# Gathers of a two-layer graph network: foreign rows passed over by a bound, and a memset of 260 columns in place of 300 ahead of each gather

## The reference, cut to what matters

```
h = relu(layernorm(x)); x = x + L0(h)     # graph attention, 8 heads of 16
h = relu(layernorm(x)); x = x + L1(h)     # q, k, v attention over edges, edge bias, layernorm
L0: e = leaky(a_src[src] + a_dst[dst]);            alpha = softmax of e over edges with one dst
    out[dst] = sum alpha * h[src]
L1: s = q[dst].k[src]/4 + edge_attr @ We + be;     attn = softmax of s over edges with one dst
    out[dst] = (sum attn * v[src]) @ Wo + bo
```

## Time and profile before

| | us |
|---|---|
| median of 3 runs | 1489.5 |
| lowest and highest | 1488.92, 1489.5 |
| the profiled execution | 1486.06 |
| its span | 1484.3 |
| POOL busy | 1190.4 |
| TensorE (PE) busy | 980.2 |
| VectorE (DVE) busy | 929.5 |
| ScalarE (ACT) busy | 636.9 |
| gathers of layer 0 start, last one | 37.98, 687.37 |
| gathers of layer 1 start, last one | 764.53, 1419.28 |

### The profile page before, as it was taken

How to read it: one execution, slowest core, us unless ns; L and a number is a source line. 1 busy time by engine, 2 the same in 40 slices (tenths; PEclk the granted TensorE clock), 3 DMA queues, 4 the chain that set the end, 5 groups by cost and what they waited for, 6 DMA issues and landing times.

```text
span 1484.3 us, 21963 instructions
## 1 busy us (share of the span) xinstructions
PE 980.2 (66%) x4985; PEld 817.4 (55%) x4985; DVE 929.5 (63%) x3002; ACT 636.9 (43%) x1699; POOL 1190.4 (80%) x1806
## 2 busy tenths in 40 slices
PE   5547557777667776676575766676676856566674
PEld 4335446656555565564355655666565746455564
DVE  6446556665665666567834666666666666666578
ACT  5624343453434434341367343444445344444404
POOL 5888888888888888884048888888888888888820
PEclk9655555555555555555686778786867688787765
DMA  6332222222223222222133333333333233333311
GB/s 141 72 69 47 71 49 53 63 71 48 70 48 70 48 69 48 63 48 75 57 112 93 89 88 90 86 89 89 90 89 88 87 89 89 89 89 87 89 29 44
DMA packets 54209, 110.41 MB, mean 74 GB/s; under 512 B 16876, under 2 KB 30848, under 8 KB 53956
## 3 DMA queue, kind: packets, MB, share of 16 engines
q0 software_dynamic: 36288, 91.12, 23.5%
q1 hardware_dynamic: 16483, 17.39, 4.3%
q10 hardware_dynamic: 1313, 0.50, 0.1%
HBM read 100.60 MB, written 8.81 MB: 74 GB/s over the span
## 4 chain that ended last, share of the span: by engine, by line
POOL 39%; issue 6%; DVE 5%; PE 3%; ACT 1%; DMA 0%; DVEq 0%; POOLq 0%; SPq 0%; ACTq 0%
POOL G L511 29%; POOL pad_i L497 10%; PE bank L851 2%; DVE halves L1074 1%; DVE acc L1432 1%; DVE PV L1405 0%; DVE mv L1081 0%; DVE G L1572 0%; DVE hn L1580 0%; DVE xs L1526 0%; DVE hn L1525 0%; DVE hn L1524 0%; PE bank L899 0%; DVE G L1569 0%; DVE hn L1523 0%
## 5 line engine op out<-in xcount | busy, mean ns | idle before, releaser
L511 POOL DMA_INDIRECT G<-table,idx_all x880 | 870.6, 989 | 143.2 <-issue 124.0
L851 PE MATMUL bank<-PV,S 128*125 128x144 f32 x1760 | 446.0, 413 | 135.8 <-DVE PV L1405 74.8
L851 PEld LDWEIGHTS bank<-PV,S 128*125 128x125 f32 x1760 | 369.5, 284 | 164.1 <-issue 121.4
L1432 DVE TENSOR_TENSOR acc<-acc,bank 125x144 f32 x880 | 259.5, 295 | 235.1 <-PE bank L851 154.8
L497 POOL MEMSET pad_i<- 1x300 int32 x880 | 297.1, 338 | 18.8 <-DMA table<-h0b 9.8
L615 ACT ACTIVATE S<-iota_n,lid 128x125 f32<-128x125 f32 x880 | 275.8, 387 | 0.5 <-DVE pen L1169 0.5
L834 PE MATMUL bank<-qe,ST 125*128 x880 | 144.5, 316 | 40.1 <-DVE prod L1225 22.7
L1405 DVE TENSOR_TENSOR PV<-G,PV 128x512 f32<-128x512 f32 x220 | 150.2, 684 | 19.6 <-issue 19.4
L619 ACT ACTIVATE S<-S,ones 128x500 f32<-128x500 f32 x220 | 156.6, 712 | 7.2
L628 ACT ACTIVATE ST<-bank 125x512 f32<-125x512 f32 x110 | 62.6, 596 | 218.7 <-PE bank L899 119.1
L834 PEld LDWEIGHTS bank<-qe,ST 125*128 125x128 f32 x880 | 126.2, 221 | 50.5 <-issue 49.5
(11 more groups left out here) (220 smaller groups left out, 1257.9 us busy)
## 6 DMA issues: line engine op xcount, KB each, us to landing
G<-table,idx_all POOLq DMA_INDIRECT x880
prod<-in_edge_attr_dram SPq DMA_DIRECT2D x8, 672.0 KB
table<-G SPq DMA_DIRECT2D x12, 224.0 KB
bias_rows<-qe SPq DMA_DIRECT2D x1, 1664.0 KB, 5.8
table<-h0b SPq DMA_DIRECT2D x8, 178.5 KB
out_dram<-G SPq DMA_DIRECT2D x8, 168.0 KB
prod<-in_edge_attr_dram SPq DMA_DIRECT2D x8, 90.0 KB
xs<-in_x_dram SPq DMA_DIRECT2D x1, 504.0 KB
```

What stands on the lines that cost most here:

```text
L511: pool.indirect_dma_start(G[:, u, v, 0:w], None, table, bass.IndirectOffsetOnAxis(ap=idx_all[:, g * GV + v:g * GV + v + 1], axis=0)).then_ ...
L851: last = pe.matmul(sums_bank(p)[0:BN, at:at + H * SLOT], S[:, ur, v, :], PV[:, v, :, :].rearrange("p h k -> p (h k)"), start=True, stop=True)
L1432: ve.tensor_tensor(a, a, o, ALU.add).then_inc(s.sem["acc_added"], 1)
```

## The change

Three edits. VectorE, once before layer 0 and after `lid` and `idx_all` are there, marks every row whose `lid` is not within 0 to 124 and adds 4096 times the partition number to its index; except on partition 0 (where that is zero) the index is then past the table's last row, 3124. It does this for visits 48 and later; those of the first three groups keep their indices. Each gather, of both layers, gets a bound of 3124 without error: a row whose index is larger is passed over, and its place in `G` keeps what was there. POOL waits once, before the fourth group of layer 0, until the indices are changed. And the memset ahead of each gather writes 260 columns.

```
+        s_masked = sem("foreign_rows_masked")
...
                     u = g % UNROLL
+                    if n == 0 and g == UNROLL:
+                        pool.wait_ge(s_masked, 1)
...
-                            space(300)
+                            space(260)
                             pool.indirect_dma_start(
                                 G[:, u, v, 0:w], None, table,
-                                bass.IndirectOffsetOnAxis(ap=idx_all[:, g * GV + v:g * GV + v + 1], axis=0)
+                                bass.IndirectOffsetOnAxis(ap=idx_all[:, g * GV + v:g * GV + v + 1], axis=0),
+                                bounds_check=NODES - 1, oob_is_err=False
                             ).then_inc(s_gath[u][j], 16)
...
             ve.wait_ge(s_bz, 16)
 
+            foreign = PV[:, :, :, :].rearrange("p v h k -> p (v h k)")[:, 0:VISITS - UNROLL * GV]
+            later = slice(UNROLL * GV, VISITS)
+            ve.tensor_scalar(CC[:, 0:1], vcol_[:, 0:1], float(P * 32), None, op0=ALU.mult).then_inc(s_v, 1)
+            n_v[0] += 1
+            then(ve.tensor_scalar(foreign, lid[:, later], 0.0, float(BN - 1), op0=ALU.max, op1=ALU.min))
+            then(ve.tensor_tensor(foreign, foreign, lid[:, later], ALU.not_equal))
+            ve.scalar_tensor_tensor(idx_all[:, later], foreign, CC[:, 0:1], idx_all[:, later], op0=ALU.mult,
+                                    op1=ALU.add).then_inc(s_masked, 1)
```

## The result

The changed kernel takes 1512.05 us (median of 4 runs, 1511.66 to 1513.05), the kernel before 1489.5 in the same comparison: ratio 1.0154, 95% interval 1.0142 to 1.0166. The prediction said 1470 and a range of 1462 to 1502; the time is 42 us above the forecast and outside the range. The profiled execution's span went from 1484.3 to 1510.4 us.

The account below looks back on a forecast made before the run. POOL's memset-and-gather cycle was taken to bound both layers: 28.8 us saved by the memset, less 8.5 for collisions and 1 for new DVE instructions, bound 0, made 19.3 us, from 1489.5 to 1470; range 1462 to 1502.

Parts of the forecast that it names:

- What bounds the kernel: POOL's cycle of memset, idle time and gather, 1.45 us, sets the pace of both layers; 864 cycles count.
- The memset of 260 columns: Ahead of each gather on POOL: 40 columns fewer save 33 ns in series, 864 times, 28.8 us less.
- The collisions: Gathers starting while DVE reads two SBUF tensors wait for its end; 8.5 us given back, 7.5 of them in layer 1.
- The new DVE instructions: Once before layer 0: near 2.1 us, hidden by DVE's wait for gathers; 1 us taken for gathers beginning under them.
- the new wait: On POOL before the fourth group of layer 0: the masked indices are ready long before, so 0.
- The bound in each gather: In every gather of both layers: the test's price and the saving on foreign rows may cancel, taken as 0.
- My ends: For the bound's effect: from 8 us saved by passed-over rows to 180 ns a gather, 155 us, lost.
- decision point of 32 ns: Lengthening of each gather by the bound above which the cycle is 1.45 us again and the gain is gone.
- Rival (a): The bound lengthens every gather, deciding above 32 ns; 1506 us at 60 ns, 1530 at 100; chance 0.29.
- (b): The gather's start ignores the memset's end, or waiting fills the shorter space: 1489 us; chance 0.09, including gather lengthening around 32 ns.
- (c): Rows return later when gathers are issued faster, and POOL waits for room in its queue: 1513 us; chance 0.03.

Follow-up runs that it names:

- e1: The kernel before with only the memset cut from 300 to 260 columns; 1472.03 us, ratio 0.9894.
- e2: The kernel before with only the bound of 3124 added to every gather, memset of 300, indices unchanged; 1529.63 us, ratio 1.0276.
- e4: The kernel before without any memset ahead of the gathers; 1334.33 us, ratio 0.8967.
- e5: The kernel before with the bound in every gather, taken from a register set once, memset of 300, indices unchanged; 1517.39 us against 1488.77.
- e9: The kernel before with 220 multiplications of gathered rows (two SBUF inputs) replaced by row sums (one SBUF input); 1463.08 us against 1489.3.
- e3: The changed kernel with the memset of 300 columns; 1530.87 us, ratio 1.0282.
- e6: The kernel before with gathers of 64 rows in place of 128, no bound, and one memset added at the start; 1484.38 us.
- e7: The kernel before with gathers of 64 rows in place of 128, with the bound, and one memset added at the start; 1506.07 us.
- e8: The changed kernel, memset of 300, with all rows from visit 48 on passed over, except on partition 0; 1523.13 us.
- e11: The changed kernel without any memset ahead of the gathers; 1368.99 us, ratio 0.9198.
- e10: The kernel before with a memset of 2 columns ahead of each gather, no bound; 1346.59 us, ratio 0.9037.

## Why the prediction was wrong

**What bounds the kernel: right.** Every edit to POOL's cycle moved the time (e1, e2, e4, e5). Only without the memset does layer 1 come to wait for DVE and PE (e4).

**The memset of 260 columns: right.** 33 ns forecast; 338 to 304 ns measured in e1, with the gather starting 0.16 us after it. I did not follow this step to its end: the earlier trace rows already showed gathers 0.30 us apart without a memset, and e4 is 10% faster than the kernel before.

**The collisions: right in kind, too small.** 8.5 us forecast, 13.7 measured in e1. Layer 1, which I had worked out (7.5), gave 3.8 by its gathers alone (19.2 to 23.0 us lost), layer 0, for which I added 1 by "an equal number at other places", gave 9.9 (14.3 to 24.2). e9 shows the cause. The estimate for layer 0 had no working behind it. DVE's step is placed by the landing of rows there too, so a gather that meets L1405 in one group meets it again in the next, and the shorter cycle moved layer 0 into such a place: the 22 gathers of 1.63 to 1.66 us in e1. I take this from their even steps of 23.6 us; no run moves DVE's work alone to show it. Its first gather of layer 1 comes 4.1 us earlier (760.40 for 764.53), where I had said 10.

**The new DVE instructions and the new wait: hidden, as forecast.** e3 and e2 differ by nothing that can be measured (1530.87 and 1529.63 us).

**The bound in each gather: the step that failed.** I wrote "A test is a small part of an index's arithmetic, and a foreign row's saving is seldom; the two may cancel. I take 0". It measures 52 to 55 ns in every gather (e2, the changed kernel), about half of it, by the estimate from e6 and e7, independent of rows, and nothing cancels, since a row passed over saves no POOL time (e8). My ends, a gain of 8 us and 180 ns a gather, held it; the value in between did not, and the gap from the decision point of 32 ns was 23 ns. Both ends came from rows of gathers without a bound, and my zero was chosen between them by opinion. The 1.4 ns a row under both ends was itself too large, taken from two different gathers at two digits; e6 gives 0.6.

**Rival (a)** was what happened. By its own formula 55 ns give 1489.5 + 23 x 0.6 = 1503; the other 9 us are about the pauses (9.8 us more idle time), which no row of before showed. Rivals (b) and (c) fell with e1 and e4. The range's top, 1502, was set by the chance I gave to (a) and not by its mechanism. A price that, if it exists at all, is paid in every one of 880 cycles deserved more than 0.29.

**Still open.** What the pauses are. With the moves and a memset of 260 or 300 columns some 0.9 us are added at about every 72nd gather of 128 rows. With the moves and no memset there are none (e11), and none without the moves and with a memset of 300 (the kernel before, e5). Without the moves and with a memset of 2 columns they are there, some 0.3 us (e10), with one of 260 columns eight gathers in the same places have 0.06 us more idle time than the others (e1), and at 64 rows they come every 84 gathers with and without moves (e6, e7). Also open are some 4 us of e2, and whether the bound's price at other numbers of rows lies on the line through 64 and 128.

## What to carry to other kernels

Where one engine's queue alone sets the pace of a loop, an option on its repeated instruction is priced by the count, here 52 ns x 880; with no row for it, its price belongs on the losing side until one run has shown it. A filler between such instructions is to be tried at zero first: 0.20 of the cycle's 1.45 us went to it for nothing. A gain estimated from the cycle alone is not safe where another engine can hold the queue: a new cycle can fall in step with that engine's work, as layer 0 of e1 did. And skipping rows pays only if the bytes were the limit.

## What the runs showed of the hardware

- A bound lengthens an indirect gather of 128 rows from 952 to 1004 ns, one of 64 rows from 914 to 953. Given as a number it also puts a MOVE of 29 ns on POOL's queue each time; given as a register it doesn't (e5: 1006 ns a gather, no MOVE).
- A row passed over is still a packet of the queue (36288 in all) and saves no POOL time, only its bytes (91.1 to 13.5 MB in e8).
- Indirect gathers of 128 rows can start every 1.25 us (e4), or 1.26 with a memset of 2 columns between them (e10); a memset counts in full only where it is longer than some 0.15 us, an estimate from the distances (0.30 apart without, 0.31 with 0.09, 0.50 with 0.34).
- A gather that starts under a VectorE instruction with two SBUF inputs waits nearly until its end (0.24 us on average for 90 gathers under L1405 in the kernel before, none for 46 under L1225). One that starts under a short instruction directly ahead of such a one can wait for both, 1.66 us in place of 0.95 (e1). Replacing 220 such instructions took 25 us off the gathers (e9). The Trainium skill's page "SBUF — State Buffer", section "Who interferes with whom", names a second SBUF input as what contends with a GpSimd instruction that reads SBUF; the runs agree, by the 25 us of e9.
